# First maxima of the first attention made inside the feed-forward part of the same layer

## The reference

```python
# layer 0, attention: 16 heads of 16, two softmaxes over causal scores
scores = einsum('bhid,bhjd->bhij', q, k) / sqrt(16)
std_out = out_proj(softmax(where(mask, scores, neg)))
splat_attn = einsum('bhin,bhjn->bhij', amp * qg, kg) + strength * einsum('bhin,bhjn->bhij', amp * qg * qd, kg * kd)
gsa_out = out_proj(softmax(where(mask, scores + sensitivity * splat_attn, neg)))
attn = (1 - blend) * std_out + blend * gsa_out
# layer 0, feed-forward: 256 -> 768 -> 256, weights rounded to fp8 values
fuse = silu((x @ gate_w) * gate_s) * ((x @ up_w) * up_s)
ffn = (fuse @ down_w) * down_s
```

## Time and profile before

| | |
|---|---|
| median of three runs | 1950.85 us |
| the profiled execution | 1951.57 us |
| its span, first to last instruction | 1949.8 us |
| TensorE busy | 1716.4 us (88%) |
| VectorE busy | 1480.2 us (76%) |
| mean granted clock of TensorE | 0.924 |

### The profile page before, as it was taken

How to read it: one execution, slowest core, us unless ns; L and a number is a source line. 1 busy time by engine, 2 the same in 40 slices (tenths; PEclk the granted TensorE clock), 3 DMA queues, 4 the chain that set the end, 5 groups by cost and what they waited for, 6 DMA issues and landing times. The chain is left out here.

```text
span 1949.8 us, 31698 instructions
## 1 busy us (share of the span) xinstructions
PE 1716.4 (88%) x10498; PEld 1194.2 (61%) x10498; DVE 1480.2 (76%) x3097; ACT 1214.9 (62%) x2737; POOL 662.4 (34%) x1294
## 2 busy tenths in 40 slices
PE   4989799999999888788789998887886899987998
PEld 3558444444444577567668876766764445546887
DVE  6765789999997358999988789998267688916454
ACT  2534278888778434788877678887541678855111
POOL 2002212122222215666666456665143111125100
PEclk9889699999999989888989998888997799987999
DMA  3463122333330200000000000000034522110001
GB/s 119 130 216 66 33 48 58 62 66 67 67 67 2 74 1 1 1 1 1 1 1 1 1 1 1 1 1 1 29 105 119 95 55 55 29 72 1 1 1 44
DMA packets 36130, 82.51 MB, mean 42 GB/s; under 512 B 9600, under 2 KB 11776, under 8 KB 34944
## 3 DMA queue, kind: packets, MB, share of 16 engines
q1 hardware_dynamic: 35968, 80.48, 16.9%
HBM read 52.79 MB, written 27.26 MB: 41 GB/s over the span
## 5 line engine op out<-in xcount | busy, mean ns | idle before, releaser
L1035 ACT ACTIVATE probs<-pss 128x512 f32<-128x512 f32 (+3 forms) x1152 | 482.2, 496 | 133.7 <-PE pss L998 132.3
L1063 DVE TENSOR_REDUCE negmax<-px 128x2 f32<-128x1024 f32 (+2 forms) x480 | 506.9, 1113 | 52.3 <-PE px L979 49.0
L1602 POOL TENSOR_SCALAR rp<-sw,tau 128x256 f32<-128x256 f32 x720 | 341.0, 504 | 7.2
L998 PE MATMUL pss<-queries,keys 64*128 64x512 f32 (+3 forms) x1152 | 298.5, 398 | 9.1 <-ACT probs L1035 5.6
L1112 POOL TENSOR_SCALAR_AFFINE_SELECT probs<-probs 128x512 f32<-128x512 f32 x192 | 120.4, 635 | 534.3 <-ACT probs L1035 534.3
L979 PE MATMUL px<-keys,queries 63*128 63x512 f32 (+3 forms) x1152 | 271.1, 429 | 13.5 <-DVE negmax L1063 13.4
L998 PEld LDWEIGHTS pss<-queries,keys 64*128 64x128 f32 x1152 | 169.1, 191 | 156.0 <-ACT probs L1035 135.1
L1012 PE MATMUL po<-probs,vals 128*32 128x512 f32 (+3 forms) x2304 | 248.2, 507 | 0.3 <-POOL probs L1112 0.2
L1451 PE MATMUL pss<-again,sw 128*128 128x256 f32 x1024 | 245.0, 398 | 0.0
L1756 DVE BATCH_NORM_STATS2 st<-rp 128x6 f32<-128x512 f32 x360 | 229.6, 675 | 2.2 <-POOL rp L1602 2.2
L1451 PEld LDWEIGHTS pss<-again,sw 128*128 128x128 f32 x1024 | 203.8, 203 | 28.7
(11 more groups left out here) (359 smaller groups left out, 2509.5 us busy)
## 6 DMA issues: line engine op xcount, KB each, us to landing
queries<-rec_q SPq DMA_DIRECT2D x96, 128.0 KB, 3.6
keys<-rec_k SPq DMA_DIRECT2D x96, 128.0 KB, 3.7
queries<-rec_q SPq DMA_DIRECT2D x96, 64.0 KB, 3.5
keys<-rec_k SPq DMA_DIRECT2D x96, 64.0 KB, 3.5
rec_q<-fs SPq DMA_DIRECT2D x16, 256.0 KB, 4.3
rec_k<-fs SPq DMA_DIRECT2D x16, 256.0 KB, 4.5
rec_q<-vals SPq DMA_DIRECT2D x16, 256.0 KB
rec_k<-vals SPq DMA_DIRECT2D x16, 256.0 KB
```

Of the source, the lines that this page charges most:

```text
L998: e.matmul(tl.pss[scores % 3][:, 512 - width:512], ops.ks[p][at:at + STACK + 1, tile, j * P:(j + 1) * P], ops.qs[p][at:at + STACK + 1, til ...
L1035: e.activation(tl.probs[arg][:, w, :], tl.pss[scores % 3][:, 512 - width:512], ACT.Exp).then_inc(self.exp_made, 1)
L1063: e.tensor_reduce(out, from_px, X_AXIS, ALU.max, negate=True).then_inc(self.x_read, 1)
L1602: x = e.tensor_scalar(self.rp[rp % 6][:, :, h], self.view(g, q)[:, h, :], -BIG, self.tau[r][:, 2 * q + h:2 * q + h + 1], ALU.min, ALU.max)
```

## The change

A new class FirstMaxima holds one px (two banks), its own negmax and rows and five semaphores. Its 20 units, the turn into a row, the copy and the sending of the row go into the feed-forward stage. The table MAXIMA says how many units a cell (i, f) gets: of two, the first stands between the gate and the up products, the other after the down products. On VectorE the first stands ahead of fz, the other between fz and fl. schedule() no longer yields the units and rows of group 0. On POOL start.clear stands before the first addition, not the fifth. The code of a unit's products and of its reduction moves into the functions maximum_products and largest_of without a change.

```diff
     SLOTS = FC + 3
+    MAXIMA = {(1, 4): 1, (1, 5): 1, (2, 0): 1, (2, 1): 1, (2, 2): 2, (2, 3): 2, (2, 4): 1, (2, 5): 1, (3, 0): 1,
+              (3, 1): 2, (3, 2): 2, (3, 3): 2, (3, 4): 2, (3, 5): 1}
...
+            first.px = k.ps("px", [P, 2, 512])
...
     def pe(self, e):
...
+                extra = iter(self.maxima(i, f))
                 if i < NB:
                     if m >= 2:
                         e.wait_ge(self.silu_made, m - 1)
                     products(e, self.pg[b][:], ...
+                    for n in islice(extra, 1):
+                        self.first.product(e, n)
                     if m >= 2:
                         e.wait_ge(self.fused, m - 1)
                     products(e, self.pu[b][:], ...
...
+                for n in extra:
+                    self.first.product(e, n)
+                if (i, f) == (NB, 1):
+                    self.first.turn(e)
+
+    def sp(self, e):
+        self.first.send(e)
...
     def dve(self, e):
...
+                for n in islice(extra, 1):
+                    self.first.largest(e, n)
                 e.wait_ge(self.silu_made, m + 1)
                 e.wait_ge(self.up_in, m + 1)
...
+            for n in extra:
+                self.first.largest(e, n)
             if m:
                 e.wait_ge(self.fh_made, m)
...
+        self.first.row(e)
+        self.first.copy(e)
         for n in range(4 * (NB - 1), 4 * NB):
             self.scale(e, n)
...
     def pool(self, e):
         k = self.k
         for n in range(NT):
-            if n == 4:
+            if n == 0:
                 self.start.clear(e)
...
+class FirstMaxima:
...
+    def product(self, e, n):
+
+        if n:
+            e.wait_ge(self.x_read, n)
+        else:
+            e.wait_ge(self.ops.loaded[0], 16 * self.ops.PARTS)
+        maximum_products(e, self.k, self.ops, 0, *self.units[n], self.px).then_inc(self.x_in, 1)
...
+    def largest(self, e, n):
+
+        e.wait_ge(self.x_in, n + 1)
+        largest_of(e, self.ops, *self.units[n], self.px, self.negmax).then_inc(self.x_read, 1)
...
     def schedule(self):
...
-        yield from self.maxima(0)
-        yield "rows", 0, None, None
+        if self.begun is None:
+            yield from self.maxima(0)
+            yield "rows", 0, None, None
...
                 if scores % 48 == 0:
-                    e.wait_ge(self.row_sent, 16 * (g + 1))
+                    if g or self.begun is None:
+                        e.wait_ge(self.row_sent, 16 * (g + 1 - self.before))
+                    else:
+                        e.wait_ge(self.begun.sent, 16)
```

More of the change, by code:

```diff
@@ L591, in __init__, with maxima @@
             "gate_in up_in silu_made fused fh_made fl_made down_in scaled added")
+    def maxima(self, i, f):
+        at = sum(c for where, c in self.MAXIMA.items() if where < (i, f))
+        return range(at, at + self.MAXIMA.get((i, f), 0))
     def pe(self, e):
@@ L785, in sp, with maximum_products @@
             t.load(self.k, e, p)
+def maximum_products(e, k, ops, g, w, arg, px):
+    width, parts = arg
+    diag = [t * P + P == c + width for t, c in parts][0]
+    fresh = not ops.adds(w)
+    if diag and fresh:
+        for side in range(2):
+            for n in range(2):
+                at = HALF * n
+                to = px[:, n, 0:len(parts) * width].rearrange("p (s k) -> p s k", k=width)
+                e.matmul(to[:, :, width - P + HALF * side:width - HALF + HALF * side],
+                         k.mask_of[at:at + HALF, side, :], k.mask_by[at:at + HALF, side, 0:len(parts), :],
+                         start=side == 0, stop=False, skip_group_check=True)
+    for s, (t, c) in enumerate(parts):
+        for n in range(2):
+            _, tile, at, _ = ops.of[w + n]
+            x = e.matmul(px[:, n, s * width:(s + 1) * width], ops.qs[g % 3][at:at + STACK, tile, t * P:(t + 1) * P],
+                         ops.ks[g % 3][at:at + STACK, tile, c:c + width], start=fresh and not diag, stop=True,
+                         skip_group_check=True)
+    return x
@@ new lines, in largest_of @@
+def largest_of(e, ops, w, arg, px, negmax):
+    width, parts = arg
+    a, b = ops.place(w), ops.place(w + 1)
+    of = slice(a, b + 1, b - a) if b > a else slice(a, None if b == 0 else b - 1, b - a)
+    if len(parts) == 2:
+        out = negmax[:, :, of, parts[0][0]]
+        from_px = px[:, :, 0:2 * width].rearrange("p n (s k) -> p s n k", s=2)
+    else:
+        (t, c), = parts
+        out = negmax[:, c // 512, of, t % 4 if c else t]
+        from_px = px[:, :, 0:width]
+    return e.tensor_reduce(out, from_px, X_AXIS, ALU.max, negate=True)
@@ L822, with __init__ @@
               (512, ((3, 0),)), (512, ((7, 512),)), (512, ((4, 0),)), (512, ((5, 0),)), (512, ((6, 0),)), (512, ((7, 0),)))
-    def __init__(self, k, operands, t, records):
+    def __init__(self, k, operands, t, records, begun=None):
         self.k, self.ops, self.t, self.records = k, operands, t, records
+        self.begun, self.before = begun, 0 if begun is None else 1
         self.order = self.ORDERS[operands.nk]
@@ L955, in pe @@
             if what == "max":
-                width, parts = arg
-                diag = [t * P + P == c + width for t, c in parts][0]
                 if g > maxed:
@@ L962, in pe @@
                     e.wait_ge(self.x_read, places - 2)
-                fresh = not ops.adds(w)
-                if fresh:
+                if not ops.adds(w):
                     std_place[arg] = places
```

89 lines of the change are left out of this document (49 added, 40 removed).

## The result

The changed kernel took 1944.73 us (median of 20 runs, 1939.23 to 1951.51), the kernel before 1948.49 in the same comparison (20 runs, 1943.06 to 1952.53). The ratio is 0.9978, with a 95% interval from 0.9970 to 0.9987: 4 us faster, where I had forecast 11.1. The profiled execution has a span of 1945.3 us, 4.5 less than before, and a mean granted clock of 0.931. So the direction was right, and more than half of the gain did not come.

The account below looks back on a forecast made before the run. TensorE was taken to bound the feed-forward part and VectorE's 20 reductions the attention's head. Gone 22.9 + 3.2 = 26.1, added 6.8 + 3.6 + 2.3 + 1.7 + 0.6 = 15.0: 11.1 us faster, 1939.8 us, range 1934 to 1946.

Parts of the forecast that it names:

- the price of a unit on TensorE: Feed-forward stage: each of the 20 moved units adds 0.34 us of products on TensorE, 6.8 in all.
- My upper bound of 9.2: Upper end for the 20 units' products: 20 x 0.46 us if the two of a pair ran one after the other.
- The waits for the one px: Feed-forward rows 2 and 3: TensorE waits for the single buffer's reductions, 3.6 us added, ends 0 and 7.3.
- the 0.7 and 0.5 for the other cells: Buffer waits: 0.7 us on entering (2,3) and (2,4), 0.5 at the heads of rows 2 and 3.
- Taking turns: Rival: VectorE and TensorE wait for each other in full in cells with two units; 6.1 us worse, 1945.9; chance 0.12.
- The first unit's operands: Cell (1,4): loads land at 160.5, TensorE comes at 158.21 and waits 2.3 us, ends 1 and 5.
- The low clock behind that wait: After the load wait in cell (1,4): 3.4 us at half clock, 1.7 us lost, ends 0 and 4.
- The first group: First attention group: 3.2 us shorter, 0.9 from the row's wait and 2.3 from ScalarE's start and low clock.
- the 22.94: Head of the first attention, 206.99 to 229.93: the 20 reductions with nothing beside them go entirely, 22.94 us.
- the clears at no cost: Feed-forward stage: POOL's four clears end by 152.7, before its first addition at 154.71, so moving them costs POOL nothing.
- full clock through rows 2 and 3: Feed-forward rows 2 and 3: TensorE keeps full clock, against the rival of a lasting low clock (1957.0, chance 0.06).
- the tail: End of the feed-forward stage: fl comes 0.3 us later and the row's transposing product costs 0.3, 0.6 added.

Follow-up runs that it names:

- e4: The changed kernel with the products of the ten standard units issued a second time directly ahead, into the same px; 1952.69 us.
- e3: The changed kernel with the products of the 20 units on all 128 rows instead of 63, maxima not the reference's; 1951.26 us.
- after: The changed kernel itself, against the kernel before; 1944.73 us, ratio 0.9978.
- e5: e1 plus 10 and 5 unused products in two waits of the feed-forward tail, so TensorE enters the attention without a pause; 1936.79 us, ratio 0.9924.
- e8: The changed kernel plus 16 unused products in cell (1,4), while TensorE waits for the first unit's loads; 1942.83 us.
- e11: e10 plus the 20 unused full-height products of e9 in the first group; 1945.96 us, ratio to the kernel before 0.9969.
- e1: The changed kernel with the same 20 units placed later, the first in cell (2,0) instead of (1,4); 1941.68 us, ratio to the kernel before 0.9955.
- e6: e1 plus one exponential of one column ending ScalarE's feed-forward list, so its table loads there; 1939.96 us, ratio 0.9947.
- e7: e1 with a cell's first unit behind the up products instead of between gate and up products; 1938.84 us, ratio 0.9940.
- e9: e5 plus one unused full-height 512-column product behind each of the 20 scores ahead of the first group's first values; 1950.43 us.
- e10: e1, e5, e6 and, for cells with down products, e7 joined; 1935.49 us, ratio to the kernel before 0.9912.
- e2: The kernel before with only POOL's four clears moved ahead of all its additions; 1949.43 us, ratio 0.9997.

## Why the prediction was right and wrong

**The step that failed is the price of a unit on TensorE: 20 x 0.34 = 6.8.** It measured 0.63 for a wide unit, 12.5 in all. The row was read rightly, but it stands in the attention, ahead of a product of the same height; the new place is between full-height products, where the weight load behind the pair does not run ahead. e4 shows the low price beside its own kind and e3 the neighbours' loads restored. My upper bound of 9.2 was computed from two products one after the other and did not think of the neighbours at all, so the true value lay outside it.

The Trainium skill ("TensorE: Matmul & The Clock Gate", Part 3: Packing small matmuls) says that two products in different row groups run concurrently, which the rows confirm, and that a weight load overlaps with running products "only when row_grp differs", though the same part names the background weight buffer as a second case. Here loads of full-height products ran ahead of one another's products all through the feed-forward part (spacing 0.23 with loads of 0.19), and only at the change between 128 and 63 rows did they not. So the quoted rule does not hold here as it stands; the measurement decides.

**The waits for the one px: 3.6 predicted, 1.1 measured.** This error hid almost half of the first one, and mostly follows from it. The loop of one px (pair, reduction, passing on) was predicted at 0.34 + 1.5 = 1.84 and measured 1.82, from 201.17 to 202.99. But the pair and the gate products, which run in this time, fill 1.55 of it and not 1.27, so 0.27 is left to wait. It came at the four places named, in cells (3,2) to (3,5); the 0.7 and 0.5 for the other cells did not come at all. "Taking turns" did not occur, VectorE is busy 32.57 of 40.

**The first unit's operands: 2.3 predicted, 3.88 measured.** The landing was right within 0.2 us. What was off is when TensorE would arrive, 1.55 us earlier in this execution. In the six profiles in which TensorE waited for the operands (after, e3, e4, e5, e8, e11) the unit could start 14.8 to 17.0 us behind the first clear; a place that depends on two chains, POOL's and DMA's against TensorE's, should have had room for both to vary. The place of e1, two cells on, had no such wait in five profiles (e1, e6, e7, e9, e10) and 1.45 and 1.00 in two (e5, e11), so even it is a little early.

**The low clock behind that wait: 1.7 predicted, 2.3 to 2.4 measured** (e8; and 6.9 - 3.88 - 0.63 = 2.4 in after). Right in kind, a little small.

**The first group: 3.2 predicted, 2.1 measured.** The wait for the row went as said. The clock did not: in the nine profiles with the opening moved and no unused products in the group it falls 1.4 to 7 us into the group and is back 3.2 to 4.3 us behind the first values products, though TensorE is 94 to 100% busy while it is down (after, e5, e10, in windows of 2 us), and it stays up with full-height products in between (e9, e11). My doubt in the earlier trace rows, that TensorE was busy and slow at 244, was this. The Trainium skill ("TensorE: Matmul & The Clock Gate", A second HAM failure mode: psum-queue depth-cycling) gives short idle times between groups of products as a cause of a clock that goes up and down. In rows 2 and 3 of this stage four such pauses of 0.20 changed nothing; in the first group the clock stays down for 12 us in which TensorE is idle for 0.04, so idle time does not keep it down there; whether idle time brought it down is open (below).

**Right:** the 22.94, the clears at no cost (e2), full clock through rows 2 and 3, the tail (0.6, measured 0.64), and that ScalarE's and VectorE's other work stays covered. Of the signs I had named, the first scores within a microsecond (0.77) and the length of the first group (25.3) came; the attention stage began 19.0 us later than before instead of 13 to 16, the waits in row 3 were 0.20 instead of 0.6, and the clock behind the load wait was low for almost 7 us instead of 3.

**The sum:** 5.7 too little for the units, 2.5 too much for the waits, 1.6 too little for the load wait, 0.7 for its clock, 1.1 for the first group, nothing for the tail: 5.7 - 2.5 + 1.6 + 0.7 + 1.1 = 6.6 us, which is 11.1 - 4.5. That 1944.73 still lies between 1934 and 1946 is luck: the kernel before took 2.4 us less in this comparison than in the three runs that I started from. 1950.85 x 0.9978 is 1946.6.

What stays open: whether it is the number of rows itself or something that goes with it (the pairs, the order of the products) that lets the clock fall; only a full-height product was put in between. It also filled the pauses at the group's head: TensorE is 68% busy from 224 to 226 in e5 and 90% from 226 to 228, just before the fall, and full in e11; so that the low clock lasts under full load is shown, that it falls without any pause is not. And the runs' ratios differ from the stretches of one profile by up to 5 us; the start of this stage moves by 7 from execution to execution, and nothing here says why.

## What to carry to other kernels

The duration of an instruction holds for its neighbours, too: before a small product is moved, look at what stands on either side of it, and count from the product ahead of it to the second one behind it. Small-height products are cheap among themselves and dear among full-height ones (0.23 to 0.34 against 0.63), so moving them in runs rather than singly should pay; no run here did that with useful work. And a consumer that is put beside a chain of loads needs as much room as that chain varies between executions, since TensorE pays for the wait twice, once in idle time and once in clock.

## What the runs showed of the hardware

- A pair on 63 rows between products on 128 rows costs 0.09 ahead of it and 0.11 behind it; the weight load does not run ahead at this place (201.60 above). It does in e3.
- TensorE's granted clock fell from 1.00 to 0.50 at about 228, behind 2 us with 68% and 2 us with 90% of work, all on 63 and 64 rows (e5), lay at 0.50 for 12 us with 11.96 of work in them (after), and stayed at 1.00 with 20 full-height products among them (e9, e11).
- 3.88 us of idle time brought 1.2 GHz from about 159 to 166 (after); 16 unused products in the same place kept it at 1.00, an idle of 1.34 us included (e8). Load waits of 1.45 (e5) and 1.00 (e11) left it at 1.00, those of 2.60 (e3) and 4.40 (e4) did not.
- A table load of ScalarE (1.28 us) ahead of the first group's exponentials was worth less than its length: 0.35 us against e1, in one profile (e6).
